# A fused two-layer vision and text block: the reciprocal roots of the first loop's layer norms, taken by POOL's power operation in place of integer seeds and Newton steps on VectorE

## The chip, the cores and the metric

The kernel runs on one core of a Trainium2 chip. The metric is the device time of one execution in microseconds (us). The engines are TensorE (PE), VectorE (DVE), ScalarE (ACT), GpSimd (POOL) and SyncE (SP), each with its own queue of instructions that it works off in order. They wait for one another by semaphores.

## The reference

Sixteen images of 224 by 224 become 196 tokens of 192 channels each and get 128 text tokens behind them: 324 tokens, `h`. Four residual blocks follow, each on a layer norm of `h`. All norms are without learned factors here; the root in question is 1 / sqrt(variance + 1e-5) of each token.

```python
def _layernorm(x, axis=-1, eps=1e-05):
    m = jnp.mean(x, axis=axis, keepdims=True)
    v = jnp.var(x, axis=axis, keepdims=True)
    return (x - m) / jnp.sqrt(v + eps)
...
h = _L0_tok_ref(x, L0_tok_W)
h = jnp.concatenate([h, txt], axis=1)
h = h + _L0_attn_ref(_layernorm(h, axis=-1), ...)   # circular convolution by softmax weights
h = h + _L0_ffn_ref(_layernorm(h, axis=-1), ...)    # gelu MLP, 192 -> 768 -> 192
h = h + _L1_attn_ref(_layernorm(h, axis=-1), ...)   # 12 heads, 324 queries on 324 + 196 shared keys
h = h + _L1_ffn_ref(_layernorm(h, axis=-1), ...)    # expert choice over 4 experts, with attention inside
```

The last block takes its own norm of its input, with an epsilon of 1e-6. So the fourth norm of `h` is followed by a norm of the normalised tile. The kernel gets both from one variance v: the first factor is 1/sqrt(v + 1e-5), the second, applied to `h` itself, 1/sqrt(v(1 + 1e-6) + 1e-5 * 1e-6).

## The kernel before, in words

A batch is one image. Its 324 tokens are three tiles of 108 partitions by 192 channels, so the variance of a norm is a tile of 108 x 3 numbers. Two attentions are the bulk: `one` (second block, with the shared keys) and `two` (inside the fourth block). The first loop runs `one` for batch i and weaves the other three blocks' steps of batches i - 1 to i + 3 between its units; the second loop does the same around `two`. Two turns (i = 15 and 16) run both.

The order of the work is written out by hand. ORDER_1 has 15 slots. `s` is a head's score product and its exponential, `m` one product and one maximum of a query tile (on VectorE, through three PSUM banks `mps`), `a` four products of probabilities and values, `r` the transposes of the finished maxima, `p` a step of the expert choice that only some batches have. The other words are steps, and OFF_1 says of which batch, relative to i. Every engine walks the same list and does its own part of each word, in that order. So a word's place in the list is its place in the queue of each engine that has a part in it.

The steps `ln1` to `ln4` are VectorE's alone before the change. Each has four parts, 0 to 3. Part 0 takes the statistics (three `bn_stats`, L1006). Part 1 combines them (`bn_aggr`, L1017), adds epsilon (L1019; ln4 also L1022 for the second root), makes an integer seed of the root (L1025) and runs one Newton step (L1011 to L1013). Part 2 runs two more. Part 3 writes the normalised tile (L1030). ln4 has its normalised tile `xna` in part 2 and, in part 3, three small operations that make the second factor (L1184 to L1186), and `xn5`. One operation that needs the result of the one before it is linked to it by a semaphore of VectorE's own (`link`).

The tiles go to TensorE's transposes: `t1` of ln1 (then `zv`, `val`, the first attention), `t2` of ln2 (then `hid`, `out`), `t3` of ln3 (then `qk`, and `v` a batch later), `t4` and `t5` of ln4 (then `log`, the router). Each waits for its norm's signal (`ln1_done` to `ln4_done`).

POOL has in this order within a batch: `hx` = ha + xna (L777, waits for ln4), `hab` (L783), `hb` (L800), a copy `hc` (L790), the parts of the queries and keys in bf16 (`parts`, L758 and L760, once for each of qk0, qk1 and qk2), and the loads of the next image (`xload`). What `parts` writes goes to DRAM and from there into `qpack` and `kpack` by SP's DMAs (`todram`, `pack0` to `pack2`), and the products `m` of the next group read them.

Of the kernel before, what the change touches and what calls it, by code (L numbers as in the profile page):

```python
# [9 lines left out]
P, T = 108, 3  # L10
# [25 lines left out]
ORDER_1 = (  # L36
# [226 lines left out]
def build(nc, A):  # L263
# [3 lines left out]
    with ctx:  # L267
        def sb(name, shape, dt=fp32):
            return ctx.enter_context(nc.sbuf_tensor(name, shape, dt))
# [45 lines left out]
        st = sb("st", [P, T, 6])  # L315
        mv = sb("mv", [P, T, 2])
        var = sb("var", [P, 2 * T])
        rs = sb("rs", [P, 2 * T])
        nt = sb("nt", [P, 2 * T])
        xT1 = sb("xT1", [KP, 2, N])  # L320
# [193 lines left out]
        ln3_done = signal("ln3_done")  # L514
        ln4_done = signal("ln4_done", 2)
        nmz_ready = signal("nmz_ready")
        zs_ready = signal("zs_ready")
# [22 lines left out]

        MEMSETS_POOL, SETUP_POOL, SETUP_DVE = 10, 14, 10
        block = ctx.enter_context(nc.Block())
# [172 lines left out]
        def _(pool):  # L715
# [6 lines left out]
            for n, (x, value) in enumerate(((of[64:KP, :, :, :], 0.0), (xS[KC:KP, :, :], 0.0), (v1[:, :, :, :], 0.0),  # L722
                                            (kpack[KC:KP, :, :], 0.0), (yA[KC:KP, :, :], 0.0),
                                            (v1[:, 0:KT1 - 1, :, D:D + 1], 1.0), (v1[0:LAST1, KT1 - 1, :, D:D + 1], 1.0),
                                            (kpack[6 * D:6 * D + 3, :, :], 1.0), (yA[KC:KC + 1, :, :], 1.0),
                                            (bc[:, :, :], 1.0))):
# [24 lines left out]
            def parts(att, ring, j, i, m):  # L751
# [3 lines left out]
                if comes_first(att, j):  # L755
# [5 lines left out]
                                        ALU.subtract).then_inc(att.third.sem, 1)  # L761

            def first_step(name, k, c, what, j, i):
                if name == "shared":
                    shared_pieces()
                    both_layers()
                elif name == "xload":

# [207 lines left out]
        def _(dve):  # L976
# [51 lines left out]
            def normalised(src, dst, scales):  # L1028
                for t in range(T):
                    done = nc.vector.tensor_scalar(dst[:, t, :], src[:, t, :], mv[:, t, 0:1], scales[:, t:t + 1],  # L1030
                                                   ALU.subtract, ALU.mult)
                return done

            def layernorm(step, src, dst, signals):

                if step == 0:
                    statistics(src)
                elif step == 1:
                    variances(T)
                    newton(T, 1)  # L1040
                elif step == 2:
                    newton(T, 2)
                else:
                    normalised(src, dst, rs).then_inc(signals.sem, 1)

# [50 lines left out]
            def first_step(name, k, c, what, j, i):  # L1096
# [8 lines left out]
                elif name == "ln1":  # L1105
                    if k == 0:
                        front.emptied(dve, i, "tok")
                        dve.wait_ge(x_in.sem, x_in.at(j, 48))
                    layernorm(k, hin, xn1, ln1_done)
                elif name == "ln2":  # L1110
                    if k == 0:
                        front.emptied(dve, i, "proj_1")
                    layernorm(k, h, xn2, ln2_done)
                elif name == "ln3":
                    if k == 0:
                        front.emptied(dve, i, "out_1")
                    layernorm(k, h, xn3, ln3_done)
                elif name == "zv":
# [53 lines left out]
                elif name == "ln4":  # L1172
                    if k == 0:
                        front.emptied(dve, i, "proj4_1")
                        statistics(ha)
                    elif k == 1:
                        variances(2 * T)
                        newton(2 * T, 1)
# [456 lines left out]
```

## Time and profile before

| | |
|---|---|
| median of 3 runs | 2161.02 us (2160.82 to 2162.99) |
| profiled execution | 2163.17 us |
| its span, first to last instruction | 2161.4 us |
| TensorE busy | 1898.0 us, 88% |
| VectorE busy | 1425.0 us, 66% |
| ScalarE busy | 1119.6 us, 52% |
| POOL busy | 267.0 us, 12% |
| mean granted clock of TensorE | 0.962 of full speed |

The profile is of one execution. Busy time is the time in which an engine has an instruction at work; TensorE's products are pipelined and their ends modelled, so a busy TensorE is not one at its peak. An instruction's row gives its start in the span, its duration, its engine and line, what it writes and reads, and in brackets how long the engine had been idle before it and which instruction ended that.

### The profile page before, as it was taken

What the parts mean: (1) busy time and instruction counts of PE and PEld (TensorE: products, weight loads), DVE (VectorE), ACT (ScalarE), POOL (GpSimd) and SP (SyncE); (2) the same over time, 40 slices, a digit from 0 to 9 for tenths busy, and PEclk for the clock granted to TensorE, in tenths of its full rate; (3) what the DMA queues carried; (4) which work ended last, traced back from release to release, by engine and by line L of the source; (5) the groups of instructions that cost most, each with busy time, mean ns of one, the idle gap of its engine ahead of it and who ended that gap; (6) DMA issues with size and microseconds to landing.
All of it is one profiled execution on the core that took longest, in us unless ns stands there. A gap on an engine that the chain in (4) does not pass through costs nothing. (4 is left out here: it accounts for less than half of the span.)

```text
span 2161.4 us, 42850 instructions
## 1 busy us (share of the span) xinstructions
PE 1898.0 (88%) x11904; PEld 1267.3 (59%) x11904; DVE 1425.0 (66%) x4566; ACT 1119.6 (52%) x2585; POOL 267.0 (12%) x406
## 2 busy tenths in 40 slices
PE   3688998998998998998998987767899999999996
PEld 2465665666665666665665654434566666666664
DVE  3267777767867867868868866524677656566563
ACT  1244554554554554554554554353565656566563
POOL 4301101101101101101101101100011001001000
PEclk9799999999999999999999999978999999999998
DMA  4202112112112112112122021302334333433431
GB/s 150 53 16 55 49 32 61 37 39 60 42 39 56 40 45 57 40 47 57 37 51 57 27 55 51 80 25 68 76 89 114 78 97 94 110 93 89 115 83 35
DMA packets 157452, 134.86 MB, mean 62 GB/s; under 512 B 31924, under 2 KB 136344, under 8 KB 157208
## 3 DMA queue, kind: packets, MB, share of 16 engines
q1 hardware_dynamic: 153592, 127.90, 22.7%
q0 software_dynamic: 2304, 4.79, 0.9%
q8 instruction: 58, 0.95, 0.2%
q10 hardware_dynamic: 1440, 0.75, 0.1%
q14 instruction: 58, 0.48, 0.1%
HBM read 81.96 MB, written 50.16 MB: 61 GB/s over the span
## 5 line engine op out<-in xcount | busy, mean ns | idle before, releaser
L1228 DVE TENSOR_REDUCE mxh<-mps 108x1 f32<-108x260 f32 (+1 forms) x1728 | 684.5, 442 | 351.2 <-PE mps L1400 340.3
L943 ACT ACTIVATE prob<-sps 108x324 f32<-108x324 f32 x1536 | 623.1, 439 | 523.5 <-PE sps L1370 477.6
L1400 PE MATMUL mps<-kpack,qpack 96*108 96x260 bf16 (+1 forms) x1728 | 420.9, 298 | 56.2 <-DMA kpack<-scr_k 25.0
L1370 PE MATMUL sps<-qpack,kpack 128*108 128x324 bf16 x1536 | 440.8, 321 | 33.4 <-ACT prob L943 26.7
L1400 PEld LDWEIGHTS mps<-kpack,qpack 96*108 96x108 bf16 x1728 | 220.5, 131 | 210.4 <-DVE mxh L1228 86.7
L1385 PE MATMUL aps<-prob,v 128*32 128x324 f32 x3072 | 318.5, 459 | 3.7 <-ACT prob L943 1.2
L1370 PEld LDWEIGHTS sps<-qpack,kpack 128*108 128x108 bf16 x1536 | 192.2, 129 | 211.8 <-ACT prob L943 149.9
L1356 PE MATMUL lin<-yT,w 128*128 128x324 f32 x576 | 186.0, 455 | 18.1 <-ACT g L843 13.7
L1356 PEld LDWEIGHTS lin<-yT,w 128*128 128x128 f32 x576 | 103.6, 194 | 63.8 <-issue 32.7
L1385 PEld LDWEIGHTS aps<-prob,v 128*32 128x32 f32 x3072 | 73.2, 110 | 105.2 <-issue 60.3
L758 POOL CAST piece<-rest 128x324 bf16<-128x324 f32 x96 | 43.6, 454 | 729.5 <-DVE rest L1060 721.9
L777 POOL TENSOR_TENSOR hx<-ha,xna 108x576 f32<-108x576 f32 x16 | 22.4, 1397 | 863.2 <-DVE xna L1030 863.2
L1356 PE MATMUL lin<-xT,w_in 128*128 128x324 f32 x384 | 119.8, 445 | 0.5 <-ACT xT L839 0.5
L1346 PE MATMUL lin<-w,g 128*108 128x192 f32 x576 | 108.0, 329 | 2.7 <-PEq L136 2.7
L1346 PE MATMUL lin<-w_out,g 128*108 128x192 f32 x576 | 108.1, 330 | 2.0 <-PEq L136 2.0
L1329 PE MATMUL lin<-ident,xn 108*96 108x108 f32 x384 | 62.2, 284 | 46.3 <-DVE xn L1030 37.5
L957 ACT COPY av<-aps 128x324 f32<-128x324 f32 x96 | 41.1, 428 | 103.2 <-PE aps L1385 78.0
L1346 PEld LDWEIGHTS lin<-w,g 128*108 128x108 f32 x576 | 91.2, 173 | 5.7 <-issue 3.4
L1346 PEld LDWEIGHTS lin<-w_out,g 128*108 128x108 f32 x576 | 92.0, 176 | 4.2 <-issue 2.5
L943 ACT ACT_TABLE_LOAD x65 | 83.4, 1283 | 14.8 <-PE sps L1370 12.9
L843 ACT ACT_TABLE_LOAD x66 | 84.7, 1283 | 8.7 <-PE lin L1356 7.6
L1356 PEld LDWEIGHTS lin<-xT,w_in 128*128 128x128 f32 x384 | 68.0, 193 | 28.2 <-ACT g L843 5.1
(157 smaller groups left out, 2402.4 us busy)
## 6 DMA issues: line engine op xcount, KB each, us to landing
qpack<-scr_q SPq DMA_DIRECT2D x96, 243.0 KB, 3.3
kpack<-scr_k SPq DMA_DIRECT2D x96, 121.5 KB, 3.3
scr_q<-piece SPq DMA_DIRECT2D x32, 243.0 KB, 3.1
scr_k<-piece SPq DMA_DIRECT2D x32, 243.0 KB, 4.0
kpack<-scr_k SPq DMA_DIRECT2D x96, 81.0 KB, 3.1
bc<-rec_d SPq DMA_DIRECT2D x128, 60.8 KB, 2.4
scr_q<-piece SPq DMA_DIRECT2D x32, 162.0 KB, 3.5
scr_q<-piece SPq DMA_DIRECT2D x64, 81.0 KB, 3.4
```

The source lines that it names most:

```text
L758: nc.gpsimd.tensor_copy(piece[:, m, 1, :], rest[:, m, :]).then_inc(att.second.sem, 1)
L777: nc.gpsimd.tensor_tensor(hx[:, :, :], ha[:, :, :], xna[:, :, :], ALU.add).then_inc(hx_ready.sem, 1)
L843: nc.scalar.activation(g[:, f, :], ring.at(i, what)[:, 0:N], ACT.Gelu, bias=b_in[:, f:f + 1] if bias else 0.0).then_inc(ring.free["act"].s ...
L943: nc.scalar.activation(prob[0:rows, n % NP, :], sps[0:rows, n % 2, 0:N], ACT.Exp, scale=SCALE).then_inc(att.exped.sem, 1)
L957: nc.scalar.copy(av[:, q, :], aps[:, 0:N]).then_inc(att.copied.sem, 1)
L1228: nc.vector.tensor_reduce(mxh[:, hd, t, s:s + 1], att.mps.at(i, use)[0:P, 0:att.width], AX.X, ALU.max, negate=True).then_inc(att.mps.free[ ...
L1329: done = nc.tensor.transpose(b[0:KC, t * P:(t + 1) * P], src[:, t, k * KC:(k + 1) * KC], ident[0:P, 0:P])
L1346: done = mm(tiles2(b)[0:P, t % 2, :], acts[k][:, t * P:(t + 1) * P], weights[k], start=k == 0, stop=k == 5)
L1356: done = mm(b[0:size, 0:N], w[:, k, c:c + size], x[:, k, 0:N], start=k == 0, stop=k == 1)
L1370: mm(sps[0:rows, n % 2, 0:N], kpack[:, 4 * q + n % 4, k * att.rows:k * att.rows + rows], qpack[:, 4 * q + n % 4, :], start=True, stop=True ...
L1385: mm(aps[32 * hd:32 * hd + 32, 0:N], att.values[:, k, 4 * q + hd, :], prob[:, n % NP, :], start=k == 0, stop=k == kt - 1).then_inc(att.sum ...
L1400: mm(bank[0:P, 0:att.width], qpack[0:6 * D, 4 * q + hd, t * P:(t + 1) * P], kpack[0:6 * D, 4 * q + hd, s * att.width:(s + 1) * att.width], ...
```

## The change

The variance of each norm goes to POOL. VectorE's part 1 is now only `bn_aggr`, which signals `spread_known`. POOL, at the same word of the list (part 1 of each norm), waits for that, adds epsilon, waits for its own result, raises to the power -0.5 and signals `root_known`. VectorE waits for that ahead of the normalisation. ln4 has two additions and one power over both roots, and its part 3 uses the second one as it is. Each norm has its own tiles for mean and variance, sum and root. Part 2 of ln1, ln2 and ln3 is empty and its words go from the list; `hx` moves behind `ln4_2` in it, three words later. POOL's setup has one more memset, the exponents.

```diff
-    "a ln2_1 m m m s v_0.0 s ln2_2 ln2_3 s s m v_0.1 m s m p v_1.0 s recip s",
+    "a ln2_1 m m m s v_0.0 s ln2_3 s s m v_0.1 m s m p v_1.0 s recip s",
...
-    "hid5 m m s s m proj4_0.0 m den m proj4_0.1 s spread0 spread1 proj4_1 s s ln4_0 a s hx ln4_1 r ln4_2 s",
+    "hid5 m m s s m proj4_0.0 m den m proj4_0.1 s spread0 spread1 proj4_1 s s ln4_0 a s ln4_1 r ln4_2 hx s",
...
-    "exp p m ln3_2 s s ln3_3 t5_1 s m m s a",
+    "exp p m s s ln3_3 t5_1 s m m s a",
...
-    "a s t1_0 t1_1 s s ln1_2 ln1_3 zv s",
+    "a s t1_0 t1_1 s s ln1_3 zv s",
...
+            def reciprocal_roots(n, j):
+
+                pool.wait_ge(spread_known[n].sem, spread_known[n].at(j, 1))
+                pool.sem_inc(gate_pool.sem)
+                nc.gpsimd.tensor_scalar(vars4[:, n, 0], mean[n][:, :, 1], EPS4, None, ALU.add).then_inc(vars_known[n].sem, 1)
+                if n == 3:
+                    nc.gpsimd.tensor_scalar(vars4[:, n, 1], mean[n][:, :, 1], 1.0 + EPS5, EPS4 * EPS5, ALU.mult,
+                                            ALU.add).then_inc(vars_known[n].sem, 1)
+                w = 2 if n == 3 else 1
+                pool.wait_ge(vars_known[n].sem, vars_known[n].at(j, w))
+                nc.gpsimd.tensor_tensor(root[n][:, 0:w, :], vars4[:, n, 0:w, :], minus_half[:, 0:w, :],
+                                        ALU.pow).then_inc(root_known[n].sem, 1)
...
-            def newton(w, times):
-                for _ in range(times):
-                    link(nc.vector.tensor_tensor(nt[:, 0:w], rs[:, 0:w], rs[:, 0:w], ALU.mult))
-                    link(nc.vector.scalar_tensor_tensor(nt[:, 0:w], nt[:, 0:w], -0.5, var[:, 0:w], ALU.mult, ALU.mult))
-                    link(nc.vector.scalar_tensor_tensor(rs[:, 0:w], nt[:, 0:w], 1.5, rs[:, 0:w], ALU.add, ALU.mult))
-
-            def variances(w):
+            def variances(n):
                 for t in range(T):
-                    done = nc.vector.bn_aggr(mv[:, t, :], st[:, t, :])
-                link(done)
-                done = nc.vector.tensor_scalar(var[:, 0:T], mv[:, :, 1], EPS4, None, ALU.add)
-                if w > T:
-
-                    done = nc.vector.tensor_scalar(var[:, T:2 * T], mv[:, :, 1], 1.0 + EPS5, EPS4 * EPS5, ALU.mult, ALU.add)
-                link(done)
-
-                link(nc.vector.tensor_scalar(rs[:, 0:w].bitcast(i32), var[:, 0:w].bitcast(i32), -0.5, 1597463007.0,
-                                             ALU.mult, ALU.add))
...
+                    done = nc.vector.bn_aggr(mean[n][:, t, :], st[:, t, :])
+                done.then_inc(spread_known[n].sem, 1)
...
                 else:
-                    normalised(src, dst, rs).then_inc(signals.sem, 1)
+                    dve.wait_ge(root_known[n].sem, root_known[n].at(j, 1))
+                    normalised(src, dst, n, root[n][:, 0]).then_inc(signals.sem, 1)
...
                     elif k == 2:
-                        newton(2 * T, 2)
-                        normalised(ha, xna, rs).then_inc(ln4_done.sem, 1)
+                        dve.wait_ge(root_known[3].sem, root_known[3].at(j, 1))
+                        normalised(ha, xna, 3, root[3][:, 0]).then_inc(ln4_done.sem, 1)
                     else:
 
-                        link(nc.vector.tensor_tensor(nt[:, 0:T], rs[:, 0:T], var[:, 0:T], ALU.mult))
-                        link(nc.vector.tensor_tensor(nt[:, 0:T], nt[:, 0:T], rs[:, 0:T], ALU.mult))
-                        link(nc.vector.tensor_tensor(nt[:, 0:T], nt[:, 0:T], rs[:, T:2 * T], ALU.mult))
-                        normalised(ha, xn5, nt).then_inc(ln4_done.sem, 1)
+                        dve.wait_ge(root_known[3].sem, root_known[3].at(j, 1))
+                        normalised(ha, xn5, 3, root[3][:, 1]).then_inc(ln4_done.sem, 1)
```

## Rows read from the trace of the kernel before

**Rows 1.** Page, part 1: busy us, share of the span, instructions of each engine.

```profile
PE 1898.0 (88%) x11904; PEld 1267.3 (59%) x11904; DVE 1425.0 (66%) x4566; ACT 1119.6 (52%) x2585; POOL 267.0 (12%) x406
```

**Rows 2.** Waits of PE, 100 to 1250 us: us in total, times, longest us.

```profile
PE lin L1329 <- DVE xn L1030: 25.2, 34, 5.3
...
PE mps L1400 <- DVE mxh L1228: 10.5, 21, 1.5
```

**Rows 3.** Timeline of PE, 404 to 463 us: start, us, what [idle before <- releaser].

```profile
413.05 0.32 PE L1400 MATMUL mps<-kpack,qpack 96*108 96x260 bf16 x1 [0.54 <-DVE mxh L1228]
...
417.33 0.48 PE L1329 MATMUL lin<-ident,xn 108*96 108x108 f32 x3 [0.42 <-DVE xn L1030]
...
425.34 0.30 PE L1410 MATMUL mps<-identb,mp 108*12 108x108 bf16 x3 [1.54 <-DVE mp L1242]
...
430.61 0.76 PE L1329 MATMUL lin<-ident,xn 108*96 108x108 f32 x6 [0.82 <-DVE xn L1030]
...
437.26 0.54 PE L1400 MATMUL mps<-kpack,qpack 96*108 96x260 bf16 x3 [1.12 <-DMA kpack<-scr_k]
...
462.51 0.48 PE L1329 MATMUL lin<-ident,xn 108*96 108x108 f32 x3 [0.51 <-DVE xn L1030]
```

**Rows 4.** Groups by line, DVE: busy us, mean ns, then idle before them.

```profile
L1011 DVE TENSOR_TENSOR nt<-rs 108x3 f32<-108x3 f32 (+1 forms) x192 | 43.7, 228 | 6.5 <-DVEq L140 1.7
L1013 DVE SCALAR_TENSOR_TENSOR rs<-nt,rs 108x3 f32<-108x3 f32 (+1 forms) x192 | 31.6, 165 | 6.6
```

**Rows 5.** Timeline of DVE, 399 to 462 us.

```profile
399.22 0.32 DVE L1017 BATCH_NORM_AGGREGATE mv<-st 108x2 f32<-108x6 f32 x3
...
401.85 0.96 DVE L1030 TENSOR_SCALAR xna<-ha,mv,rs 108x192 f32<-108x192 f32 x3
...
404.07 0.33 DVE L1184 TENSOR_TENSOR nt<-rs,var 108x3 f32<-108x3 f32 x1
404.43 0.51 DVE L1185 TENSOR_TENSOR nt<-nt,rs 108x3 f32<-108x3 f32 x1
...
410.38 0.30 DVE L1017 BATCH_NORM_AGGREGATE mv<-st 108x2 f32<-108x6 f32 x3
...
412.57 1.10 DVE L1228 TENSOR_REDUCE mxh<-mps 108x1 f32<-108x260 f32 x3
...
416.24 0.96 DVE L1030 TENSOR_SCALAR xn<-h,mv,rs 108x192 f32<-108x192 f32 x3
...
429.52 0.96 DVE L1030 TENSOR_SCALAR xn<-hin,mv,rs 108x192 f32<-108x192 f32 x3
...
457.78 0.31 DVE L1017 BATCH_NORM_AGGREGATE mv<-st 108x2 f32<-108x6 f32 x3 [0.55 <-DVE st L1006]
...
461.42 0.96 DVE L1030 TENSOR_SCALAR xn<-h,mv,rs 108x192 f32<-108x192 f32 x3
```

**Rows 6.** Timeline of POOL, 402 to 427 us.

```profile
402.98 1.40 POOL L777 TENSOR_TENSOR hx<-ha,xna 108x576 f32<-108x576 f32 x1 [51.92 <-DVE xna L1030]
404.34 1.68 POOL L783 TENSOR_TENSOR hab<-hc,b_p 108x192 f32<-108x192 f32 x3
...
426.52 0.80 POOL L760 TENSOR_TENSOR piece<-rest,piece 128x324 bf16<-128x324 f32 x1
```

**Rows 7.** Groups by line and form, POOL, whole span.

```profile
L800 POOL TENSOR_TENSOR hb<-hin,b_p 108x192 f32<-108x192 f32 x48 | 27.0, 588 | 67.0 <-issue 30.3 <-ACT hin L882 29.8 <-ACTq L140 6.8
...
L729 POOL MEMSET kpack<- 32x6240 bf16 x1 | 5.3, 5292 | 0.1
...
L1625 POOL MEMSET const-float32-0.0<- 128x1 f32 x1 | 0.1, 103 | 0.4 <-issue 0.4
```

**Rows 8.** Timeline of PE at the start.

```profile
101.26 1.32 PE L1329 MATMUL lin<-ident,xn 108*96 108x108 f32 x6 [5.35 <-DVE xn L1030]
```

**Rows 9.** Timeline of DVE at the start, the first ln3.

```profile
80.65 0.32 DVE L1017 BATCH_NORM_AGGREGATE mv<-st 108x2 f32<-108x6 f32 x3 [0.40 <-DVEq L140]
...
85.25 0.96 DVE L1030 TENSOR_SCALAR xn<-h,mv,rs 108x192 f32<-108x192 f32 x3
```

More of the change, by code:

```diff
@@ L315, in build @@
         st = sb("st", [P, T, 6])
[L316 to L319, printed above, removed]
+        mean = [sb(f"mean{n}", [P, T, 2]) for n in range(4)]
+        root = [sb(f"root{n}", [P, 2, T]) for n in range(4)]
+        vars4 = sb("vars4", [P, 4, 2, T])
+        minus_half = sb("minus_half", [P, 2, T])
         xT1 = sb("xT1", [KP, 2, N])
@@ L515, in build @@
         ln4_done = signal("ln4_done", 2)
+        spread_known = [signal(f"ln{n + 1}_spread") for n in range(4)]
+        root_known = [signal(f"ln{n + 1}_root") for n in range(4)]
+        vars_known = [signal(f"ln{n + 1}_vars", 2 if n == 3 else 1) for n in range(4)]
         nmz_ready = signal("nmz_ready")
@@ L539, in build @@
         gate_pe, gate_pool, gate_sp = signal("gate_pe", 0), signal("gate_pool", 0), signal("gate_sp", 0)
-        MEMSETS_POOL, SETUP_POOL, SETUP_DVE = 10, 14, 10
+        MEMSETS_POOL, SETUP_POOL, SETUP_DVE = 11, 15, 10
         block = ctx.enter_context(nc.Block())
@@ L766, in first_step @@
                     both_layers()
+                elif name in ("ln1", "ln2", "ln3", "ln4"):
+                    if k == 1:
+                        reciprocal_roots(number(name) - 1, j)
                 elif name == "xload":
@@ L1007, in statistics, with normalised, layernorm @@
                 link(done)
-            def newton(w, times):
-                for _ in range(times):
-                    link(nc.vector.tensor_tensor(nt[:, 0:w], rs[:, 0:w], rs[:, 0:w], ALU.mult))
-                    link(nc.vector.scalar_tensor_tensor(nt[:, 0:w], nt[:, 0:w], -0.5, var[:, 0:w], ALU.mult, ALU.mult))
-                    link(nc.vector.scalar_tensor_tensor(rs[:, 0:w], nt[:, 0:w], 1.5, rs[:, 0:w], ALU.add, ALU.mult))
-            def variances(w):
-                for t in range(T):
-                    done = nc.vector.bn_aggr(mv[:, t, :], st[:, t, :])
-                link(done)
-                done = nc.vector.tensor_scalar(var[:, 0:T], mv[:, :, 1], EPS4, None, ALU.add)
-                if w > T:
-                    done = nc.vector.tensor_scalar(var[:, T:2 * T], mv[:, :, 1], 1.0 + EPS5, EPS4 * EPS5, ALU.mult, ALU.add)
-                link(done)
-                link(nc.vector.tensor_scalar(rs[:, 0:w].bitcast(i32), var[:, 0:w].bitcast(i32), -0.5, 1597463007.0,
-                                             ALU.mult, ALU.add))
-            def normalised(src, dst, scales):
+            def variances(n):
+                for t in range(T):
+                    done = nc.vector.bn_aggr(mean[n][:, t, :], st[:, t, :])
+                done.then_inc(spread_known[n].sem, 1)
+            def normalised(src, dst, n, scales):
                 for t in range(T):
-                    done = nc.vector.tensor_scalar(dst[:, t, :], src[:, t, :], mv[:, t, 0:1], scales[:, t:t + 1],
+                    done = nc.vector.tensor_scalar(dst[:, t, :], src[:, t, :], mean[n][:, t, 0:1], scales[:, t:t + 1],
                                                    ALU.subtract, ALU.mult)
                 return done
-            def layernorm(step, src, dst, signals):
+            def layernorm(step, j, n, src, dst, signals):
                 if step == 0:
@@ L1038, in layernorm @@
                 elif step == 1:
[L1039 to L1042, printed above, removed]
-                else:
-                    normalised(src, dst, rs).then_inc(signals.sem, 1)
+                    variances(n)
+                else:
+                    dve.wait_ge(root_known[n].sem, root_known[n].at(j, 1))
+                    normalised(src, dst, n, root[n][:, 0]).then_inc(signals.sem, 1)
             def residual(ring, i, what, k, dst, add):
@@ L1108, in first_step @@
                         dve.wait_ge(x_in.sem, x_in.at(j, 48))
-                    layernorm(k, hin, xn1, ln1_done)
+                    layernorm(k, j, 0, hin, xn1, ln1_done)
                 elif name == "ln2":
@@ L1112, in first_step @@
                         front.emptied(dve, i, "proj_1")
-                    layernorm(k, h, xn2, ln2_done)
+                    layernorm(k, j, 1, h, xn2, ln2_done)
                 elif name == "ln3":
@@ L1116, in first_step @@
                         front.emptied(dve, i, "out_1")
-                    layernorm(k, h, xn3, ln3_done)
+                    layernorm(k, j, 2, h, xn3, ln3_done)
                 elif name == "zv":
@@ L1176, in first_step @@
                     elif k == 1:
-                        variances(2 * T)
-                        newton(2 * T, 1)
+                        variances(3)
                     elif k == 2:
-                        newton(2 * T, 2)
-                        normalised(ha, xna, rs).then_inc(ln4_done.sem, 1)
-                    else:
-                        link(nc.vector.tensor_tensor(nt[:, 0:T], rs[:, 0:T], var[:, 0:T], ALU.mult))
-                        link(nc.vector.tensor_tensor(nt[:, 0:T], nt[:, 0:T], rs[:, 0:T], ALU.mult))
-                        link(nc.vector.tensor_tensor(nt[:, 0:T], nt[:, 0:T], rs[:, T:2 * T], ALU.mult))
-                        normalised(ha, xn5, nt).then_inc(ln4_done.sem, 1)
+                        dve.wait_ge(root_known[3].sem, root_known[3].at(j, 1))
+                        normalised(ha, xna, 3, root[3][:, 0]).then_inc(ln4_done.sem, 1)
+                    else:
+                        dve.wait_ge(root_known[3].sem, root_known[3].at(j, 1))
+                        normalised(ha, xn5, 3, root[3][:, 1]).then_inc(ln4_done.sem, 1)
                 elif name == "log":
```

2 lines of the change are left out of this document (1 added, 1 removed).

## The prediction

> **What bounds the kernel now.** I read four views in this order. The page's first part says that TensorE is busy 88% of the span, VectorE 66% and POOL 12% [rows 1]. No stage but the start has TensorE waiting for long, so what counts is the short waits. The list of waits gives them for 100 to 1250 us, which is 14 batches of the first loop: TensorE waits 25.2 us for normalised tiles and 10.5 us for the row maxima (VectorE empties the `mps` banks) [rows 2]. The timeline of TensorE shows where they lie in a batch [rows 3], here one batch from its `hx` at 402.98 us on. The reader should see six waits. The one at 413.05 (0.54) is for a maxima bank, the one at 417.33 (0.42) for ln3, 425.34 (1.54) for the last maxima's chain of five small operations, 430.61 (0.82) for ln1, 437.26 (1.12) for the DMA that fills `kpack`, and 462.51 (0.51) for ln2. ln4 has no wait of its own: TensorE has the `out` products to do.
>
> **What is removed.** Per batch VectorE loses 11 operations in each of ln1, ln2 and ln3 (variance, seed, nine of Newton) and 15 in ln4 (two variances, seed, nine, and three for the second root): 48, or 768 in 16 batches. The 576 of Newton are 43.7 + 31.6 + 31.6 us, since L1012 has the same count and sum as L1013 [rows 4]. The other 192 are between 0.16 us each, as L1013, and 0.51, as L1185 beside POOL [rows 4, 5], so 31 to 98 us. VectorE loses 140 to 205 us of 1425. That is no gain by itself, since it isn't the bound; it is worth what the waits above lose.
>
> **What is added.** POOL gets per batch 5 additions or scalings and 4 powers on 3 elements a partition (6 for ln4), each power behind a wait on POOL's own result. VectorE gets five waits, two of them in ln4, of which the second finds its root long there. One root costs: hand-over from VectorE to POOL 0.17 (xna ends 401.85 + 0.96 = 402.81, `hx` starts 402.98 [rows 5, 6]); the addition; POOL's wait on itself; the power; the hand-over back. No row shows a power on POOL or a 3-element tensor operation. From below each is 0.10 us (the memset of one element), from above 5.29 us (the longest single instruction on POOL) [rows 7]. Both ends hold for the power. The addition is of the kind of L800, which takes 0.59 us for 192 elements [rows 7], so it lies near the low end: I take 0.2. For the power I take the nearest row by engine, partitions and two tensor inputs, L800's 0.59, as the price of a slow function on few elements. The two hand-overs inside POOL and back I take at 0.1 each, from the 0.17. Root R = 0.17 + 0.2 + 0.1 + 0.6 + 0.1 = 1.2 us, and 1.4 for ln4 with its second addition. With the power at its ends R is 0.7 and 5.9.
>
> **Each norm with R = 1.2.** [rows 3, 5, 6]
> - ln4: from the end of bn_aggr (399.54) to xna (401.85) it is 2.3 us now and 1.4 then; nothing of VectorE's lies between, so it idles for 1.4. Behind the queued wait are xna and the maxima; the banks are three deep and show no wait there. Later the three operations of ln4_3 go (0.33 from 404.07, then two of 0.51, 1.4 us with their gaps). VectorE, full here, comes 2.3 us earlier to its two additions of `h`, but TensorE does not wait for it.
> - ln3: bn_aggr ends 410.68, then 11 linked operations run in two parts, the first ahead of three maxima at 412.57. These can start 1.8 us earlier, so the wait of 0.54 at 413.05 goes. xn3 can start after log and two more maxima, some 2 us before 416.24, so the 0.42 goes. R may be 4 us before it is late.
> - ln1: POOL is on the pieces until 426.52 + 0.80 = 427.32 [rows 6], so the root is there at about 428.3 and xn1 1.2 us before 429.52. The 0.82 at 430.61 goes, but the next wait is for the DMA, whose chain begins with the same pieces on POOL, ahead of the root in POOL's order. So 1.12 becomes 1.94 and nothing is gained.
> - ln2: bn_aggr ends 458.09, xn2 starts 461.42: 3.33 us, in which VectorE also does maxima. POOL is idle, the root is there after 1.2, xn2 is some 1.9 earlier, and the 0.51 goes.
> - The unchanged waits stay: 1.54 at 425.34 is TensorE, copies and maxima in turn, without a norm.
> - Moves: `hx` stands behind the root on POOL, and SP's store of it behind that; both have a batch of time. `hb` and the copy to `hc` queue behind ln3's root, some 2 us later than now, and are needed only by the next projection. The added memset of 6 elements and its wait are 0.1 to 0.2 us beside the loads.
>
> **The sum.** The two waits of [rows 2] are 35.7 us. I take off 5.35, the start's own [rows 8], and ln1's 13 of 0.82 = 10.7, which the DMA takes back. That leaves 19.7 for 14 batches, 1.4 a batch; with 0.54 + 0.42 + 0.51 the single batch gives 1.47. For 15 batches it is 21. At the start nothing covers the norms: TensorE waits 5.35 us at 101.26 [rows 8], and about as long for the two norms before it. The ln3 there takes 85.25 - 80.97 = 4.3 us from bn_aggr to xn [rows 9], and R cuts it by 3.1; for ln2 before it and ln1 behind it I take ln4's uninterrupted 2.3 less 1.2, so 1.1 each. That is 5. In all 26 us. The profiled execution took 2163.17 us (span 2161.4, 1.8 around it), so 2137; it stands 2.15 above the median of the runs, 2161.02, from which I get 2135.
>
> **A rule of the skill weighed.** Beside POOL's `hab` (404.34) L1185 takes 0.51 us for 3 elements, while alone such an operation takes 0.17 [rows 4 to 6]. The Trainium skill (Advanced Engine Details and Errata, GPSIMD Details) says that POOL and VectorE share a read and a write interface, in conflict where VectorE reads two SBUF tensors; the trace agrees. By that rule the new POOL operations take such time from VectorE too, at most 0.35 per meeting. They would meet mostly VectorE's idle wait or reductions from PSUM, so the sum stays; if all four met something, it would be 1.4 a batch on VectorE and still not on TensorE.
>
> The Trainium skill (GPSIMD Engine Reference, Instruction dispatch) says that the first call of a freshly loaded POOL kernel costs about 6 us with no visible instruction. No run here shows it. By it, if the power were such a function, the first ln1 would be that much later and the total would be 2141 instead of 2135.
>
> **The rivals.**
> 1. The power is slow (chance 0.17), and the kernel gets slower. Three elements cost so little by count that only a function worked out lane by lane would do it. For it: no row shows it, and the end is 5.29. Against it: every row of POOL arithmetic is in steps of nanoseconds an element. At 5.29 us ln4 loses 6.1 - 2.3 - 1.4 = 2.4 a batch, ln2 5.9 - 3.3 = 2.6, ln1 3.5 less the 1.12 of DMA = 2.4, and ln3 (5.9 for its 5.56) 0.3, less the 0.54 of the maxima's wait, which goes all the same: some 7 a batch, 105 in 15, and 10 at the start: about 2275. It decides where the power passes about 3.2 us: there ln2 (R of 3.33 is what it has now), ln1 and ln4 are all as late as they are now, and only ln3's gain is left.
> 2. The waits form again (0.16). ScalarE's exponentials, 0.3 to 0.6 a time between the same products, become the last arrival when VectorE no longer is. For it: TensorE is already close to full and ScalarE sits in the same alternation. Half of the 21 goes: 2146.
> 3. ln1's wait is not taken back (0.07). If the DMA chain gets shorter with less in front of it, 0.82 x 13 = 11 us more: 2124.
> 4. The power costs 2.5 to 3.2 us, or the waits named were never last (0.06): 2157 to 2165, no change.
> The forecast has 0.54, with its own range of 2124 to 2146.
>
> **How the numbers follow.** A measurement of this kernel can tell 0.2%, 4.3 us, from no change. Faster by more: 0.54 + 0.16 + 0.07 = 0.77; within: 0.06; slower: 0.17. The range runs from 2114, below rival 3, to 2163, which takes in rivals 2 and 4 and leaves out rival 1 and a little below.
>
> **What would show it.** The row of the power on POOL: under 2 us right, over 3.2 wrong. TensorE's waits for xn should fall to near none outside the start, those for maxima to under half, and the wait for `kpack` should grow by some 0.8 a batch; if it doesn't grow, the ln1 step is wrong. VectorE busy should be 1220 to 1285 us. The batch period (`hx` to `hx`) should be 1.4 us shorter. If waits for `prob` on TensorE grow by over 0.7 a batch, it is rival 2.

## The result and the profile after

The changed kernel takes 2106.02 us (median of 4 runs, 2103.81 to 2113.02) beside 2162.01 for the kernel before on the same chip: ratio 0.9746, interval 0.9722 to 0.9771. That is 55 us less. Forecast were 26, and the time lies 8 us below the range. The profiled execution took 2107.3 us (span 2105.6); its mean granted clock is 0.961, as before (0.962), so the clock does not explain the difference between the two profiles.

The engines' totals, after, answer [rows 1]:

```profile
PE 1878.9 (89%) x11904; PEld 1263.6 (60%) x11904; DVE 1283.0 (61%) x3798; ACT 1116.7 (53%) x2585; POOL 351.6 (17%) x551
```

VectorE lost 142 us and 768 instructions, POOL gained 85. The waits of TensorE after, 100 to 1250 us (us in total, times, longest), answer [rows 2]:

```profile
PE sps L1370 <- ACT prob L962: 21.9, 59, 1.1
PE mps L1400 <- DMA kpack<-scr_k: 15.7, 11, 2.1
PE mps L1410 <- DVE mp L1242: 12.3, 8, 1.5
...
PE lin L1329 <- DVE xn L1035: 4.8, 1, 4.8
...
PE mps L1400 <- DVE mxh L1228: 1.7, 7, 0.3
```

The 34 waits for a normalised tile are one, the start's; those for maxima went from 10.5 us to 1.7. That is 29 us of waits for 55 of time. By the totals, TensorE's idle time fell by 36.7 us (span less busy, 263.4 to 226.7) and its busy time by 19.1, for the same 11904 products at the same clock. So part of the waiting had been booked as busy. Where, is in the starts of the products. First some more rows of the kernel before, around two of the waits in [rows 3]:

```profile
411.30 1.22 PE L1502 MATMUL lin<-w_r,xTa 96*108 96x4 f32 x12
...
416.63 0.28 PE L1400 MATMUL mps<-kpack,qpack 96*108 96x260 bf16 x1
...
459.32 0.34 PE L1370 MATMUL sps<-qpack,kpack 128*108 128x324 bf16 x1 [0.44 <-ACT prob L943]
459.72 0.32 PE L1400 MATMUL mps<-kpack,qpack 96*108 96x260 bf16 x1
...
461.54 0.46 PE L1370 MATMUL sps<-qpack,kpack 128*108 128x324 bf16 x2
```

And the same products after, in the batch whose `hx` is at 391.31:

```profile
399.45 1.21 PE L1502 MATMUL lin<-w_r,xTa 96*108 96x4 f32 x12
...
400.52 0.30 PE L1400 MATMUL mps<-kpack,qpack 96*108 96x260 bf16 x1
...
403.92 0.28 PE L1400 MATMUL mps<-kpack,qpack 96*108 96x260 bf16 x1
404.04 0.44 PE L1329 MATMUL lin<-ident,xn 108*96 108x108 f32 x3
...
444.83 0.34 PE L1370 MATMUL sps<-qpack,kpack 128*108 128x324 bf16 x1 [0.45 <-ACT prob L962]
445.01 0.28 PE L1400 MATMUL mps<-kpack,qpack 96*108 96x260 bf16 x1
...
446.79 0.46 PE L1370 MATMUL sps<-qpack,kpack 128*108 128x324 bf16 x2
447.09 0.44 PE L1329 MATMUL lin<-ident,xn 108*96 108x108 f32 x3
```

Read starts against starts. At ln3's second wait it was 416.63 to 417.33, 0.70 us, with "0.42 idle"; it is 403.92 to 404.04, 0.12. So the wait was worth 0.58, not 0.42: idle is counted from the modelled end of the product before, 0.28 us after its start, but without a wait the next one starts 0.12 after it. At ln3's first wait (411.30 to 413.05 against 399.45 to 400.52) 0.68 stand for an idle of 0.54. At ln2 it is 0.97 against 0.30, so 0.67 for 0.51. And at 459.32 to 459.72 there is a wait that has no bracket at all: 0.40 against 0.18 after, too short to reach beyond the modelled end. So ln2 gives 0.67 + 0.22, not 0.51.

VectorE after: the bn_aggr and the normalised tile of ln4, ln1 and ln2, and behind ln4's the tile `xn5` and the addition of `h` (answers to [rows 5]):

```profile
387.69 0.31 DVE L1030 BATCH_NORM_AGGREGATE mean<-st 108x2 f32<-108x6 f32 x3
390.18 0.96 DVE L1035 TENSOR_SCALAR xna<-ha,mean,root 108x192 f32<-108x192 f32 x3 [2.18 <-POOL root L776]
...
392.51 1.51 DVE L1035 TENSOR_SCALAR xn<-ha,mean,root 108x192 f32<-108x192 f32 x3
393.94 0.55 DVE L1052 TENSOR_TENSOR h<-lin,h 108x384 f32<-108x384 f32 x1
...
412.38 0.30 DVE L1030 BATCH_NORM_AGGREGATE mean<-st 108x2 f32<-108x6 f32 x3
415.19 0.96 DVE L1035 TENSOR_SCALAR xn<-hin,mean,root 108x192 f32<-108x192 f32 x3 [1.58 <-POOL root L776]
...
443.30 0.31 DVE L1030 BATCH_NORM_AGGREGATE mean<-st 108x2 f32<-108x6 f32 x3 [0.57 <-DVE st L1025]
445.07 0.96 DVE L1035 TENSOR_SCALAR xn<-h,mean,root 108x192 f32<-108x192 f32 x3 [0.48 <-POOL root L776]
```

`xn5` and the addition in the kernel before, in the batch of [rows 5]:

```profile
405.53 1.18 DVE L1030 TENSOR_SCALAR xn<-ha,mv,nt 108x192 f32<-108x192 f32 x3
406.64 0.54 DVE L1049 TENSOR_TENSOR h<-lin,h 108x384 f32<-108x384 f32 x1
```

The first ln3 at the start, after, VectorE and then POOL (an answer to [rows 9]):

```profile
84.11 0.31 DVE L1030 BATCH_NORM_AGGREGATE mean<-st 108x2 f32<-108x6 f32 x3 [0.40 <-DVEq L140]
85.85 1.77 DVE L1035 TENSOR_SCALAR xn<-h,mean,root 108x192 f32<-108x192 f32 x3 [1.42 <-POOL root L776]
```

```profile
85.78 1.71 POOL L819 TENSOR_TENSOR hb<-hin,b_p 108x192 f32<-108x192 f32 x3
```

POOL by line and form after, in answer to [rows 7] (busy us, mean ns, then idle before them):

```profile
L776 POOL TENSOR_TENSOR root<-vars,minus_half 108x3 f32<-108x3 f32 x48 | 42.4, 884 | 4.0
L776 POOL TENSOR_TENSOR root<-vars,minus_half 108x6 f32<-108x6 f32 x16 | 21.6, 1351 | 1.3
L770 POOL TENSOR_SCALAR vars<-mean 108x3 f32<-108x3 f32 x64 | 15.0, 235 | 922.0 <-DVE mean L1030 922.0
L772 POOL TENSOR_SCALAR vars<-mean 108x3 f32<-108x3 f32 x16 | 3.2, 197 | 1.3
```

### The profile page after: what moved, and what is told of

It is laid out like the page before. It is cut to its first block and busy times, and to the rows that moved or that the text cites. A ratio compares the mean times of both kernels' runs of the same rounds, so it can differ in the third digit from the quotient of the medians.

```text
span 2105.6 us, 42314 instructions
## 1 busy us (share of the span) xinstructions
PE 1878.9 (89%) x11904; PEld 1263.6 (60%) x11904; DVE 1283.0 (61%) x3798; ACT 1116.7 (53%) x2585; POOL 351.6 (17%) x551
## 3 DMA queue, kind: packets, MB, share of 16 engines
q0 software_dynamic: 2304, 4.79, 0.9%
## 5 line engine op out<-in xcount | busy, mean ns | idle before, releaser
L1400 PE MATMUL mps<-kpack,qpack 96*108 96x260 bf16 (+1 forms) x1728 | 416.1, 295 | 43.3 <-DMA kpack<-scr_k 22.3
L770 POOL TENSOR_SCALAR vars<-mean 108x3 f32<-108x3 f32 x64 | 15.0, 235 | 922.0 <-DVE mean L1030 922.0
L962 ACT ACT_TABLE_LOAD x65 | 83.4, 1283 | 15.8 <-PE sps L1370 13.9
L862 ACT ACT_TABLE_LOAD x66 | 84.7, 1283 | 7.3 <-PE lin L1356 6.3
L1063 DVE TENSOR_TENSOR rest<-lin,piece 128x324 f32<-128x324 f32 x96 | 47.2, 492 | 59.8 <-ACT piece L872 26.9
```

What stands on the lines that cost most here:

```text
L770: nc.gpsimd.tensor_scalar(vars4[:, n, 0], mean[n][:, :, 1], EPS4, None, ALU.add).then_inc(vars_known[n].sem, 1)
L862: nc.scalar.activation(g[:, f, :], ring.at(i, what)[:, 0:N], ACT.Gelu, bias=b_in[:, f:f + 1] if bias else 0.0).then_inc(ring.free["act"].s ...
L962: nc.scalar.activation(prob[0:rows, n % NP, :], sps[0:rows, n % 2, 0:N], ACT.Exp, scale=SCALE).then_inc(att.exped.sem, 1)
L1063: nc.vector.tensor_tensor(rest[:, m, :], ring.at(i, what)[:, 0:N], piece[:, m, 0, :], ALU.subtract).then_inc(ring.free["dve"].sem, 1)
L1400: mm(bank[0:P, 0:att.width], qpack[0:6 * D, 4 * q + hd, t * P:(t + 1) * P], kpack[0:6 * D, 4 * q + hd, s * att.width:(s + 1) * att.width], ...
```

## The experiments

All ratios are to the kernel before in the same set of runs, with 95% intervals. Each set ran on one chip, but not all sets on the same one. In all kernels with single norms `hx` stays where the change puts it; no run moves it alone. The batches' steps named below are distances between the starts of TensorE's products, the median over ten batches.

**One norm alone.** Only one norm takes its root from POOL; the others keep VectorE's chain and their words in the list.

```diff
+POOLED = (1,)          # (2,), (3,), (4,)
-                    if k == 1:
+                    if k == 1 and number(name) in POOLED:
                         reciprocal_roots(number(name) - 1, j)
...
+                elif n + 1 not in POOLED:
+                    # the bn_aggr, seed and Newton steps of the kernel before
```

Expected of ln1 alone: 

> Only ln1 takes its root from POOL; ln2 to ln4 keep seed and Newton on VectorE. Theory as predicted (the DMA for kpack takes the wait back): 0 to 3 us off 2162, the start's share alone. Theory A (each removed wait of TensorE counts from start to start, about 0.15 more than the idle time shown, and the DMA does not take it back): 0.9 a batch for 13 batches and 1 at the start, 12 to 13 us, 2149. Theory B (the gain follows the VectorE time removed, whichever wait it lies at): ln1's share of the 142 us removed, 11 of 48 operations, so 13 us, 2149. In the trace A wants zv some 0.9 us sooner after the first row transposes.

Of ln2 alone: 

> Only ln2 takes its root from POOL. As predicted: 0.51 a batch and 1.1 at the start, 9 us, 2153. Theory A: 0.67 to 0.9 a batch and 1.1 at the start, 11 to 14 us, 2149. Theory B: 13 us, 2149.

Of ln3 alone: 

> Only ln3 takes its root from POOL. As predicted: 0.96 a batch and 3.1 at the start, 17 us, 2145. Theory A: 1.3 to 1.5 a batch and 3.1 at the start, 22 to 25 us, 2138. Theory B: 13 us as the other two, 2149.

Of ln4 alone: 

> Only ln4 takes its roots from POOL, 15 VectorE operations fewer a batch, and VectorE waits 2.2 us for the root, as long as its own chain took. As predicted and by theory A: no wait of TensorE lies there, so 0 to 4 us, 2160. Theory B: 15 of 48 operations, 18 us, 2144. This is the run that tells A from B.

Measured: 2209.6 us (ratio 1.0187, 1.0174 to 1.0201), 2201.62 (1.0156, 1.0142 to 1.0170), 2191.7 (1.0112, 1.0098 to 1.0127) and 2163.62 (0.9983, 0.9969 to 0.9998). Three are slower than the kernel before. The trace shows one place for it. The first loop's code is written out for its first three and its last six turns; the eight in between are a real loop, with seven branches back to its head, and an idle time stands behind each of these. VectorE of ln1 alone, then TensorE of the same:

```profile
390.38 0.31 DVE L1040 BATCH_NORM_AGGREGATE mean<-st 108x2 f32<-108x6 f32 x3 [4.42 <-remote]
```

```profile
392.33 0.32 PE L1441 MATMUL mps<-kpack,qpack 96*108 96x260 bf16 x1 [3.93 <-DVE mxh L1269]
```

The bn_aggr is the first work behind the loop's branch. The page counts 92 packets of VectorE's instruction loads there, and 58 in the kernel before. ln4 alone has no such idle time. It was to tell the theories apart: 0 to 4 us if the waits of TensorE count, 18 if the gain follows the VectorE time removed. It gave 3.7, so the second theory is out. For the other three the suspicion was that a cost of code loading hangs on where the loop lies in VectorE's program. Counted in instructions, waits and branches included, it lies at 431 to 748 and 441 to 758 in the three with the idle, at 464 to 792 before, 464 to 777 with ln4 alone, 385 to 665 in the changed kernel.

**The same with the loop put back to 464**, by waits that are long fulfilled (two of them share an instruction):

```diff
             dve.wait_ge(setup_dve.sem, SETUP_DVE - 1)
+            for _ in range(66):      # 46 for ln2 and ln3, 158 in the changed kernel
+                dve.wait_ge(setup_dve.sem, SETUP_DVE - 1)
```

> Only ln1 takes its root from POOL, and VectorE has 33 instructions more ahead of its first loop (waits on a semaphore that is long there), so that the loop begins at instruction 464 of VectorE's program, where it began in the kernel before, and ends at 781. Theory A (the time of the ablation without them, 2209.6, was code loading at the loop's end, by where the loop lies): the idle of 4.4 us ahead of the ln2 bn_aggr in the loop is gone, and the time is that of the kernel before less what ln1 is worth: 0 to 4 us if the DMA that fills kpack takes the 0.9 us back, 2158 to 2162 beside 2162; 14 us if not, 2148. Theory B (the norm's root on POOL slows the loop for a reason of its own): still 2205 to 2212.

> Only ln2 takes its root from POOL, VectorE's first loop begins at instruction 464 by 23 added waits. Theory A (code loading was the cost of the ablation without them): no idle of 4.4 us, ln2 is worth 0.9 a batch, 13 us in 15, 2146 to 2151 beside 2162. By the prediction's own term, 0.51 a batch: 2154. Theory B (the norm itself slows the loop): 2198 to 2205.

> Only ln3 takes its root from POOL, VectorE's first loop begins at instruction 464 by 23 added waits. Theory A (code loading): no idle of 4.4 us or more at the loop's end, ln3 is worth 1.4 a batch and 3 at the start, 24 us, 2136 to 2140 beside 2162. By the prediction's own term, 0.96 a batch and 3.1: 2145. Theory B: 2188 to 2195.

> The changed kernel with 79 waits ahead of VectorE's first loop, so that it lies at 464 to 744 of VectorE's program in place of 385 to 665. Nothing of the work changes. If the slower ablations (loops at 431 to 748 and 441 to 758) were slower by where the loop ends in the program, this kernel gets the idle of 4.4 us in each of its 7 looped turns: 2106 + 31 = 2137, and the row of instruction loads in the page goes from 55 packets to over 80. If it is where the loop begins (464 as before the change), or nothing of the kind: 2106 and 55 packets.

Measured: ln1 alone 2161.02 us (0.9996, 0.9984 to 1.0008), ln2 alone 2160.16 (0.9986, 0.9970 to 1.0002), ln3 alone 2133.95 (0.9865, 0.9845 to 0.9885), the changed kernel 2109.18 (0.9749, 0.9731 to 0.9767). The idle is gone in all three ablations, and by the ratios 41, 37 and 53 us with it (the idle itself was 29 to 30 us in each). Theory A of code loading holds. Why ln3 lost more than the others by it is open. For ln1 it came out as expected with the DMA taking the gain back; ln3 gave more than its 24; ln2 missed its 13. The changed kernel did not slow down, so the end of the loop doesn't decide by itself. It is at 2106 to 2109 with the loop at 385 and at 464.

**The changed kernel with its loop at 441 to 721**, by 112 such waits. 

> The changed kernel with 56 waits ahead of VectorE's first loop, which then lies at instructions 441 to 721. Slow loops lay at 431 to 748 and 441 to 758, quick ones at 385 to 665, 401 to 690, and 464 to 744 and beyond. If the begin decides, the idle of 4.4 us is back in 7 turns: 2137 and over 80 packets of instruction loads. If it is the begin and the end together (or the length), none: 2106 and 55 to 58 packets.

Measured: 2143.14 us (0.9931, 0.9906 to 0.9955), 37 to 40 us slower than the changed kernel (by the times, by the ratios) for 56 instructions that wait for nothing. The idle is 29.4 of it; the step from `v0` to `hid`, where it falls, is 5.3 to 6.6 us longer after each of the seven branches. The first row is a wait of VectorE in it, 98 to 1222 us; the next two stand on its page (packets, MB, share) and on the page of the changed kernel:

```profile
DVE mean L1032 <- remote: 29.4, 7, 4.5
```

```profile
q14 instruction: 91, 0.75, 0.1%
```

```profile
q14 instruction: 55, 0.45, 0.1%
```

So the begin matters, but there is no idle at 464 with ends of 744 to 792, nor at 385 with 665, and there is at 441 with 721. One rule that fits all is blocks of 256 instructions with a boundary between 442 and 464, and the next 256 further, between 698 and 720. The loops without the idle (385 to 665, 401 to 690, 464 to 792) touch two blocks, those with it (431 to 748, 441 to 758, 441 to 721) three. The Trainium skill (Runtime: NRT & Kernel Launch, Instruction fetch mechanics) says that an engine holds two blocks of 256 instructions and that a taken branch to code outside them waits for its fetch. The traces agree with that: the idle of 3.7 to 4.5 us stands right behind the taken branch, and some 5 more packets are loaded for each. Where the blocks' boundaries are is inferred; a rule by the loop's begin alone, slow from somewhere above 401 to somewhere below 464, fits these kernels as well.

**One norm taken back.** The changed kernel with one norm on VectorE again, all loops from 464 on.

```diff
+POOLED = (2, 3, 4)     # (1, 3, 4), (1, 2, 4), (1, 2, 3)
```

> The changed kernel with ln1 back on VectorE's seed and Newton steps; VectorE's loop begins at instruction 464 by 46 added waits and ends at 755. Theory A (the terms add: 0.9 a batch for 13 to 15 batches, 1 at the start): 13 us slower than the changed kernel's 2109 with such waits, 2122. Theory B (what ln1 gave alone, 0.6 us): 2110. The prediction (ln1 worth nothing in the batches, 1.1 at the start) says as B.

> The changed kernel with ln2 back on VectorE; 56 added waits, loop at 464 to 755. Theory A (the step from v0 to hid is 1.0 us longer in each of 14 or 15 batches, 1 at the start): 15 us slower, 2124. Theory B (what ln2 gave alone, 1.5 us): 2111. The prediction's 0.51 a batch: 2117.

> The changed kernel with ln3 back on VectorE; 56 added waits, loop at 464 to 755. Theory A (1.5 a batch from log to the first row transposes, 3 at the start): 25 us slower, 2134. Theory B (single effects as measured, 27.6): 2137. The prediction's 0.96 a batch and 3.1: 2126. Two of these together (ln3 with ln1) would be shown if it is over 2142: then ln3's wait hides part of what ln1 or ln2 is worth.

> The changed kernel with ln4 back on VectorE; 79 added waits, loop at 464 to 759. Theory A (0.2 a batch and 1 at the start): 4 us slower, 2113. The prediction (nothing in the batches, 1.1 at the start): 2110. If VectorE's load around ln4 (15 operations of some 3 us, ahead of the two additions of h and ln3) is what uncovers the others, over 2117.

Measured: 2106.71 us (0.9761, 0.9747 to 0.9774), 2119.81 (0.9821, 0.9796 to 0.9846), 2133.18 (0.9875, 0.9860 to 0.9890), 2115.32 (0.9794, 0.9770 to 0.9817). With 0.9749 of the changed kernel so padded, times 2161:

| | ln1 | ln2 | ln3 | ln4 | sum |
|---|---|---|---|---|---|
| worth with the other three, us | 2.6 | 15.6 | 27.2 | 9.7 | 55 |
| worth alone, us | 0.9 | 3.0 | 29.2 | 3.7 | 37 |

Those of the upper row are uncertain by some 5 to 7 us each, those of the lower by 3 to 4. The upper row adds up to what the change gives (54 with the loop so padded), but the sum is uncertain by some 18, since 0.9749 stands in it four times. For ln2 and ln3 the theory of start to start comes nearest (15 and 25 expected), for ln1 the DMA that takes it back. ln4's 9.7 lies over both forecasts of it.

The granted clock bears on this table. Its mean over the executions was 0.960 in the changed kernel so padded, and 0.965, 0.963, 0.958 and 0.965 with ln1, ln2, ln3 and ln4 back. Among the 23 executions of the kernel before in one set, a hundredth more went with 4 us less (a line fitted to them), among the twelve of ln2 alone with 9. So a few us of each entry can be the clock. The same goes for the whole: the kernel before had 0.955 to 0.956 in these sets, which is some 2 to 4 of the 55 us.

The steps that move, in us:

| step | before | after | ln1 back | ln2 back | ln3 back | ln4 back |
|---|---|---|---|---|---|---|
| router products `log` to first row transposes (ln3) | 14.13 | 12.57 | 12.56 | 12.55 | 14.33 | 12.72 |
| `prt` to `zv` (ln1) | 6.12 | 5.22 | 6.12 | 5.21 | 5.22 | 5.20 |
| `zt` to first `dft` (kpack's DMA) | 2.30 | 2.41 | 1.83 | 2.14 | 2.68 | 2.27 |
| `v0` to `hid` (ln2) | 8.30 | 7.30 | 7.29 | 8.30 | 7.29 | 7.30 |
| `out` to the next `tok` (ln4) | 7.94 | 7.75 | 7.75 | 7.75 | 7.75 | 7.94 |
| mean period | 81.94 | 78.58 | 78.64 | 79.13 | 80.79 | 78.89 |

The medians hide one thing: ln2's step is 1.0 us shorter in the looped batches and only 0.6 in the last five, so it gives 14 us in fifteen batches. And the step from `zt` to `dft` scatters by itself, from 0.71 to 3.24 us in the changed kernel, so that differences of its medians under 0.5 say little.

Each norm moves its own step, whatever the others do. ln1 wins 0.9 at `zv` and its period is the same without it: with ln1 back TensorE waits less for the DMA (100 to 1250 us, ln1 back):

```profile
PE lin L1372 <- DVE xn L1058: 14.5, 11, 5.4
...
PE mps L1443 <- DMA kpack<-scr_k: 10.9, 11, 1.5
```

ln1's waits for xn are back with 9.1 us (14.5 less the start's 5.4), and kpack's fell from 15.7 to 10.9. ln1 alone, with the loop at 464, shows the same from the other side:

```profile
PE mps L1443 <- DMA kpack<-scr_k: 22.4, 14, 2.5
...
PE lin L1372 <- DVE xn L1058: 15.1, 23, 4.8
```

Beside the kernel before, the waits for xn fell by 10.1 us (25.2 to 15.1) and those for kpack grew by 8.3 (14.1 to 22.4), and the time stayed the same within its interval.

ln2 alone wins its 1.0 at `hid` too (8.29 to 7.29), but not in the time. Its stage, 100 to 1300 us (us, busy and instructions of PE, PEld, DVE, ACT, POOL, granted clock, DMA share, GB/s), for the kernel before, for ln2 alone and for the changed kernel:

```profile
100.00:1300.00 1200.00, 1082.35 (x7021) 736.84 (x7022) 891.12 (x3068) 628.30 (x1484) 148.66 (x237) 0.97 0.18 46
```

```profile
100.00:1300.00 1200.00, 1097.03 (x7042) 745.31 (x7043) 871.93 (x2922) 628.80 (x1486) 167.69 (x269) 0.95 0.18 46
```

```profile
100.00:1300.00 1200.00, 1101.31 (x7272) 755.14 (x7273) 796.06 (x2493) 645.30 (x1538) 233.07 (x380) 0.98 0.19 48
```

TensorE is busy 14.7 us longer for 21 more products, at a mean granted clock of 0.95 of 2.4 GHz in place of 0.97. The changed kernel has 0.98 in the same stretch. That is the size of the gain missing, and the clocks of all executions bear it out. ln2 alone had 0.950 on average over its twelve, the kernel before 0.956 over its 23. The two of the twelve with the highest clock (0.956 and 0.957) took 2146.42 and 2151.85 us, 10 to 15 under the kernel before. The ten others (0.946 to 0.952) took 2157.43 to 2164.75. By a line through the twelve, ln2 alone would take some 2152 us at the clock of the kernel before. So ln2's gain is there, 9 us or more, and in most executions a lower clock takes it back. Why the clock was lower is open. With ln4 alone it is 0.96 in that stretch.

**The power twice**: POOL raises to the power a second time, into a spare tile, ahead of the one that counts.

```diff
                 pool.wait_ge(vars_known[n].sem, vars_known[n].at(j, w))
+                nc.gpsimd.tensor_tensor(spare[:, 0:w, :], vars4[:, n, 0:w, :], minus_half[:, 0:w, :], ALU.pow)
```

> The changed kernel with each power on POOL done twice, the first into a spare tile: the root arrives 0.88 us later (ln4 1.35). By the timeline ln2 and ln3 have more slack than that, ln1's transposes were ready 0.1 us after the tile, so ln1 loses 0.8 a batch if the DMA does not cover it, and ln4 1.3 a batch of VectorE time in front of the maxima, 0 to 0.5 of it seen. As predicted: up to 3.2 us of power no slower than before, here at most 10 us over 2106. Theory A: ln1's 0.8 x 13 = 10 and ln4's up to 7: 2110 to 2123.

Measured: 2135.46 us (0.9865, 0.9848 to 0.9882), 26 us of the gain lost for 0.88 us more a norm and 1.35 in ln4. The steps say where: `out` to `tok` 7.75 to 8.76 (ln4), `prt` to `zv` 5.22 to 5.94 (ln1); ln2's stays at 7.30, and ln3's moves 0.2. That is more than either theory had (2110 to 2123). ln4 costs 1.0 a batch where up to 0.5 was expected, and the waits for maxima are back with it, from 1.7 to 11.5 us (100 to 1250).

**A root almost for nothing**: the kernel before with the seed alone. It leaves the Newton steps and ln4's three small operations out, so its roots are rough.

```diff
-                    newton(T, 1)
...
-                    newton(T, 2)
+                    pass
```

> The kernel before with its Newton steps and ln4's three operations left out, so the roots are the integer seeds alone: VectorE keeps the variance and the seed and POOL has nothing of it. It shows what the change would give with a root in about 0.6 us. Theory A: the waits of the norms are all gone at R = 1.3 already, ln1 gains a little more than in the changed kernel, 2098 to 2106. Theory B (VectorE time): it removes 24 us less of VectorE's than the change but no idle wait of 2.2 us in ln4 is added, 2090 to 2100.

Measured: 2096.47 us (0.9690, 0.9677 to 0.9702). The seed is there 0.5 us (ln4) to 1.1 us (ln3, where POOL works beside it) after bn_aggr, where the root from POOL takes 2.2 and 1.4. So a root that comes 0.3 to 1.7 us sooner, on VectorE itself, is worth 12 us more, give or take 6. The time lies inside theory B's range and 1.5 us under theory A's; it doesn't tell them apart.

**The image's load held back** until the first `dft` products are done, in the kernel before and in the changed one.

```diff
                     front.filled(pool, i, "tok")
+                    front.filled(pool, i, "dft_0")
```

> The kernel before, with the loads of the next image on POOL's DMA queue held until the first Fourier product of the batch, that is until kpack is filled. Theory C (in the kernel before, these 292 KB start 5.9 us after the row transposes and share the DMA engines with the loads of qpack and kpack, and the change moved them 1 us forward, which shortened kpack's wait and let ln1's gain through): kpack's wait of some 1.2 us a batch falls by 0.5 or more, 7 to 15 us off 2162. Rival (the loads do not matter to kpack): within 3 us of 2162 and kpack's wait as it was.

> The changed kernel with the same hold on the loads of the next image. Theory C: kpack's wait, 1.4 us where it occurs, falls too, 5 to 12 us off 2106, and the result is a faster kernel than both. Rival: within 3 us of 2106.

Measured: 2152.03 us (0.9948, 0.9931 to 0.9965) and 2097.47 (0.9704, 0.9690 to 0.9718). The second is 9 us faster than the changed kernel, the fastest here that computes all. The waits for kpack (100 to 1250 us) go from 14.1 us to 0.9 in the kernel before, and from 15.7 to 12.5 in the changed one. From the issue of the load of `qpack` to the first product it is 5.58 and 5.36 us with the image's load beside it, 4.84 and 4.59 without (means over twelve batches). So the image's load makes qpack's and kpack's some 0.75 us slower, and part of the wait for kpack was the image. That they share the DMA engines is the reading I give it. The other half of theory C, that the change let ln1's gain through in this way, doesn't hold: kpack's waits did not fall by the change.

## Why the prediction was wrong

- **The sizes of the waits: wrong, and this is most of the error.** The period fell by 3.4 us (81.94 to 78.58), not by 1.4. "The two waits of [rows 2] are 35.7 us ... That leaves 19.7 for 14 batches, 1.4 a batch" took idle for time. ln3's "0.54 + 0.42" measured 0.68 + 0.58 in its batch and 1.56 as a median; worth 27.2 us with its part at the start, where the sum had 0.96 x 15 + 3.1 = 17.5. ln2's "0.51" measured 0.67 and another 0.22 that no view lists, 1.0 as a median in the looped batches; worth 15.6, where the sum had 8.8. These two are 17 of the missing 29 us; ln4 below is 10 more.
- **ln4: wrong.** "Nothing in the batches". R is 2.18 us (388.00 to 390.18), not 1.4, against 2.3 before, since the power of six elements is 1.35 us. It gives 0.2 a batch from `out` to `tok` and 0.1 elsewhere, 4 us, and 3.7 to 9.7 in the time. The reason is likely that VectorE comes to its additions of `h` earlier. From the end of bn_aggr it is 7.10 us before (399.54 to 406.64) and 5.94 after (388.00 to 393.94), mainly because the three operations of ln4_3 are gone. No run takes that apart from the rest of ln4. That TensorE "does not wait for it" was read from brackets, and such small waits have none.
- **ln1: right.** Worth 2.6 us with the start's, within the noise of nothing, and the reason was right: kpack's DMA takes it back. The sign I gave, kpack's wait longer by 0.8 a batch, does not show in the changed kernel (14.1 to 15.7 us in all). It shows where ln1 alone is changed: 8.3 us in 14 batches, 0.6 each. With ln2, ln3 or ln4 alone those waits are 10.9, 11.2 and 10.4, and with ln1 back 10.9. So the other norms shorten what ln1 lengthens, and a sign must be taken between kernels that differ in that step only.
- **Not foreseen:** with ln1 back, the step from `zt` to `dft` is 0.47 shorter than before (0.3 by the mean of all fifteen batches, 1.72 beside 2.01), and the issue of `qpack`'s load comes 6.07 us after the row transposes there, 6.47 before. That would be some 4 to 6 us in 15 batches. But ln2, ln3 and ln4 alone have 1.97, 1.82 and 2.03 for that step, each as short as the three together. So it comes with any one of them, or with what all these kernels share, such as the place of `hx`. What sets it stays open.
- **The price of the root: right within its bounds.** 0.88 us where I took 0.6, the addition 0.24 for 0.2; R of the first ln3, where VectorE waits for nothing else, is 1.43 for 1.2 (84.42 to 85.85). VectorE's 1283 us is within 1220 to 1285. The first power on POOL, at 24.54 us, starts 0.09 after the addition: what I cited of a first call by the Trainium skill (GPSIMD Engine Reference, Instruction dispatch) did not occur for this operation.
- **The start: too large.** Its waits of 5.34, 6.02 and 5.35 us became 4.23, 4.09 and 4.79. That is 1.1, 1.9 and 0.6, 3.6 together, where the sum had 1.1, 3.1 and 1.1. ln1's root stands behind the pieces on POOL there. In ln3 the root came as forecast, but the normalised tile takes 1.77 us beside POOL's `hb` in place of 0.96. The whole, from the profiles: the first `hx` comes 5.2 us earlier (238.3 to 233.1), the next 13 batches give 44.2 (3.4 each), what lies behind them 6.4: 55.8. The 5.2 are mostly batches too. ln1's transposes at 101.26 come at 102.10 after, because TensorE's first product starts 2.8 us later there (15.68 and 18.46; it varies from 14.7 to 18.6 among all the profiles here).
- **POOL beside VectorE: the price was right, the place was not.** The prediction let the new operations on POOL slow VectorE by at most 0.35 us where they meet. In the rows looked at, VectorE waits or reduces maxima while they run. What costs it time is `hab` and `hb`, which now fall beside normalised tiles, with 0.27 us more for each of a tile's three operations. `xn5` takes 27.3 us in all batches together after and 20.7 before, 0.4 a batch.
- **The rivals.** The slow power (1) is out: it is far from 3.2 us. From the power twice, 26 of 55 us for 0.9 more, I estimate the break-even at a power of some 2.7 us, if it goes on in proportion. The waits re-formed (2) little: those for `prob` went from 18.9 to 21.9 us, 0.2 a batch. Rival 3 named 2124, nearest to the result, by a mechanism that didn't occur.

## What to carry to other kernels

Price a wait by the distance of two starts, and take off the distance of the same two without a wait from another batch; the idle in the brackets is short by the modelled end of what came before, and waits shorter than that are not listed. Before an ablation is believed, look whether idle "remote" appears right behind a loop's branch: where the loop lay cost 37 to 53 us here, more than most changes give, and some padding ahead of it tells. Look also at the clock of every execution and not only of the profiled one: it hid ln2's gain. What a transfer takes back is best shown by undoing that one step in the final kernel.

## What the runs showed of the hardware

- A power on POOL takes 0.88 us for 3 elements a partition and 1.35 for 6, on 108 partitions; an addition of 3 takes 0.20 to 0.24.
- VectorE's loop at an unlucky place in its program idles 3.7 to 4.5 us at each taken branch, 29.4 us in seven for the changed kernel, which got 37 to 40 us slower by it. The kernel before and the changed one both lie well, by chance.
- Three tensor_scalar operations of 192 elements on VectorE take 0.96 us alone and 1.5 to 1.8 beside an addition of two tensors on POOL.
- The granted clock in the first loop's stage (100 to 1300 us) lay between 0.95 and 0.99 in kernels with nearly the same work. Over whole executions ln2 alone had 0.950 and the kernel before 0.956 on average, and that was worth about as much as the norm.
